# Eight instead of four PE transposes per PSUM tile and VectorE copy in a linear-attention and mixture-of-experts layer

## The reference

```python
qkv = silu(hidden_states @ qkv_w.T)
q, k, v = split(qkv.reshape(b, s, H, 3 * D), 3, axis=-1)   # blocks of 256 tokens
def step(state, blk):
    qi, ki, vi = blk
    aw = einsum('bhid,bhjd->bhij', qi, ki) * dd
    intra = einsum('bhij,bhjd->bhid', aw, vi)
    inter = einsum('bhid,bhde->bhie', qi * qd_, state)
    new_state = state * bd_ + einsum('bhsd,bhse->bhde', ki * kd_, vi)
    return (new_state, intra + inter)
attn = rmsnorm(attn, norm_w)
out = (sigmoid(hidden_states @ gate_w.T) * attn) @ out_w.T
```

## Time and profile before

| what | us |
|---|---|
| two timed runs | 5248.16 and 5294.14, median 5271.15 |
| the profiled execution, device time | 4658.65 |
| its span, slowest core (0) | 4656.1 |
| spans of the other cores | 4646.3 to 4655.0 |
| layer norm, from the first sum to the last copy (core 0) | 24 to 209 |
| the four groups | 209 to about 1245 |
| experts and store | about 1880 to 4656 |

### The profile page before, as it was taken

How to read it: one execution, slowest core, us unless ns; L and a number is a source line. 1 busy time by engine, 2 the same in 40 slices (tenths; PEclk the granted TensorE clock), 3 DMA queues, 4 the chain that set the end, 5 groups by cost and what they waited for, 6 DMA issues and landing times.

```text
span 4656.1 us, 43812 instructions; the slowest of 8 cores (4646.3 to 4656.1 us)
## 1 busy us (share of the span) xinstructions
PE 3917.6 (84%) x17686; PEld 1753.4 (38%) x18010; DVE 827.2 (18%) x1373; ACT 593.8 (13%) x691; POOL 251.0 (5%) x477
## 2 busy tenths in 40 slices
PE   1386876768649953999999999999999999999996
PEld 0132332323314421444444444444444444444443
DVE  3313122130222125011011011011011011010012
ACT  3311101111121030110110110110100100100100
POOL 0000000000000000000000000000000000000000
PEclk9996876868759965999999999999999999999997
DMA  3211111112103410444444444444444444444443
GB/s 104 68 32 19 31 29 20 31 19 50 32 0 64 72 54 14 73 73 77 74 75 74 77 73 74 76 73 76 75 73 77 73 73 73 77 73 77 75 71 95
DMA packets 75331, 284.48 MB, mean 61 GB/s; under 512 B 9814, under 2 KB 9975, under 8 KB 71038
## 3 DMA queue, kind: packets, MB, share of 16 engines
q0 software_dynamic: 67216, 243.39, 31.0%
q1 hardware_dynamic: 7918, 38.29, 2.3%
HBM read 516.55 MB, written 8.39 MB: 113 GB/s over the span
## 4 chain that ended last, share of the span: by engine, by line
PE 82%; DVE 8%; issue 4%; ACT 3%; DMA 2%; DVEq 0%; ACTq 0%; SPq 0%; POOL 0%; POOLq 0%
PE PD L368 28%; PE PE L368 27%; PE PD L1041 10%; PE PE L1041 9%; PE PT L383 2%; DVE awT L640 2%; DMA ring<-i_wup 1%; PE PC L654 1%; PE PE L654 1%; DVE statc L405 1%; PE PC L1077 1%; PE PC L812 1%; ACT R L447 1%; DVE k_tm L389 1%; ACT R L674 1%
## 5 line engine op out<-in xcount | busy, mean ns | idle before, releaser
L368 PE MATMUL PD<-R,ring 128*128 128x512 bf16 x5772 | 1314.0, 383 | 30.5 <-ACT R L998 10.8
L368 PE MATMUL PE<-R,ring 128*128 128x512 bf16 x5762 | 1299.6, 380 | 9.5 <-ACT bcB L772 1.3
L368 PEld LDWEIGHTS PD<-R,ring 128*128 128x128 bf16 x5888 | 580.1, 99 | 742.3 <-issue 70.5
L368 PEld LDWEIGHTS PE<-R,ring 128*128 128x128 bf16 x5888 | 577.4, 98 | 703.6 <-issue 17.2
L1041 PE MATMUL PD<-R,ring 128*128 128x512 bf16 x2008 | 458.6, 384 | 29.4 <-DVE R L1025 21.0
L1041 PE MATMUL PE<-R,ring 128*128 128x512 bf16 x2006 | 449.5, 379 | 3.1 <-DMA ring<-i_wdn 0.6
L1018 DVE TENSOR_TENSOR R<-R 128x1024 bf16<-128x1024 bf16 x128 | 88.6, 692 | 1628.2 <-ACT R L1011 1628.2
L1041 PEld LDWEIGHTS PD<-R,ring 128*128 128x128 bf16 x2048 | 201.1, 99 | 279.4 <-issue 48.7
L1041 PEld LDWEIGHTS PE<-R,ring 128*128 128x128 bf16 x2048 | 199.7, 98 | 243.9 <-issue 4.8
L998 ACT ACTIVATE R<-PD,bupP 128x1024 bf16<-128x1024 f32 x56 | 62.4, 1114 | 1050.4 <-PE PD L368 925.9
L383 PE MATMUL PT<-ident_b,R 128*128 128x128 bf16 x256 | 37.4, 301 | 154.7 <-ACT R L447 120.0
(11 more groups left out here) (168 smaller groups left out, 1633.5 us busy)
## 6 DMA issues: line engine op xcount, KB each, us to landing
ring<-i_wup POOLq DMA_DIRECT2D x112, 512.0 KB, 5.0
ring<-i_wgt POOLq DMA_DIRECT2D x112, 512.0 KB, 5.0
ring<-i_wdn POOLq DMA_DIRECT2D x112, 512.0 KB, 5.0
xstage<-i_xm SPq DMA_DIRECT2D x16, 1024.0 KB, 4.7
ring<-i_wk POOLq DMA_DIRECT2D x16, 512.0 KB, 5.0
xstage<-i_xp SPq DMA_DIRECT2D x8, 1024.0 KB, 4.8
ring<-i_wv POOLq DMA_DIRECT2D x16, 512.0 KB, 5.0
ring<-i_wq POOLq DMA_DIRECT2D x16, 512.0 KB, 5.0
```

Source lines behind the costliest of these rows:

```text
L368: t.matmul(P[:, hh * 512:(hh + 1) * 512], sl[:, kc * 128:(kc + 1) * 128], rb[:, kc * 1024 + hh * 512:kc * 1024 + (hh + 1) * 512], start=st ...
```

## The change

Every call of `transpose_batch` gets 8 pieces instead of 4, so that one batch fills `PT` and one DVE copy takes all of it. There are half as many batches. Nothing else differs. One of the three places in the groups and the layer norm:

```diff
-              for q4 in range(4):
+              for q8 in range(2):
                   transpose_batch(
-                      R3, [lo + (q4 * 4 + j) * 128 for j in range(4)], ("lntm", k), (),
-                      lambda tc=tc, q4=q4, dst=dst: dst.ap().rearrange(
-                          "p (fc t) -> p fc t", t=1024)[:, q4 * 4:(q4 + 1) * 4,
+                      R3, [lo + (q8 * 8 + j) * 128 for j in range(8)], ("lntm", k), (),
+                      lambda tc=tc, q8=q8, dst=dst: dst.ap().rearrange(
+                          "p (fc t) -> p fc t", t=1024)[:, q8 * 8:(q8 + 1) * 8,
                                                         tc * 128:(tc + 1) * 128],
                       dst_key, ident_b)
...
-        for mcl in range(4):
-            for q4 in range(2):
-                transpose_batch(
-                    k_fm, [mcl * 1024 + (q4 * 4 + j) * 128 for j in range(4)],
...
+        for mcl in range(4):
+            transpose_batch(
+                k_fm, [mcl * 1024 + j * 128 for j in range(8)],
+                ("kf", g, mcl), pref_done,
+                lambda mcl=mcl: k_tm.ap().rearrange(
+                    "p (tc j) -> p tc j", j=512)[:, 0:8,
+                                                 mcl * 128:(mcl + 1) * 128],
+                "ktm", ident_b)
```

More of the change, by code:

```diff
@@ L489, in build_nc @@
             evp = project(slab, skey, R2, "R2", tmp_fm, ("tm", mcl), mcl * 1024)
-            pend += [lambda q4=q4, mcl=mcl, evp=evp: transpose_batch(
-                tmp_fm, [mcl * 1024 + (q4 * 4 + j) * 128 for j in range(4)],
+            pend += [lambda mcl=mcl, evp=evp: transpose_batch(
+                tmp_fm, [mcl * 1024 + j * 128 for j in range(8)],
                 ("tm", mcl), (evp,),
-                lambda q4=q4, mcl=mcl: k_tm.ap().rearrange(
-                    "p (tc j) -> p tc j", j=512)[:, q4 * 4:(q4 + 1) * 4,
+                lambda mcl=mcl: k_tm.ap().rearrange(
+                    "p (tc j) -> p tc j", j=512)[:, 0:8,
                                                  mcl * 128:(mcl + 1) * 128],
-                "ktm", ident_b) for q4 in range(2)]
+                "ktm", ident_b)]
         for mcl in range(4):
@@ L505, in build_nc @@
             evp = project(slab, skey, R2, "R2", tmp_fm, ("tm", mcl), mcl * 1024)
-            pend += [lambda q4=q4, mcl=mcl, evp=evp: transpose_batch(
-                tmp_fm, [mcl * 1024 + (q4 * 4 + j) * 128 for j in range(4)],
+            pend += [lambda mcl=mcl, evp=evp: transpose_batch(
+                tmp_fm, [mcl * 1024 + j * 128 for j in range(8)],
                 ("tm", mcl), (evp,),
-                lambda q4=q4, mcl=mcl: v_tm.ap().rearrange(
-                    "p (tc j) -> p tc j", j=512)[:, q4 * 4:(q4 + 1) * 4,
+                lambda mcl=mcl: v_tm.ap().rearrange(
+                    "p (tc j) -> p tc j", j=512)[:, 0:8,
                                                  mcl * 128:(mcl + 1) * 128],
-                "vtm", ident_b) for q4 in range(2)]
+                "vtm", ident_b)]
         for th in pend:
@@ L559, in build_nc @@
         for mcl in range(4):
-            for q4 in range(2):
-                transpose_batch(
-                    k_fm, [mcl * 1024 + (q4 * 4 + j) * 128 for j in range(4)],
[L563 to L574, removed]
+            transpose_batch(
+                k_fm, [mcl * 1024 + j * 128 for j in range(8)],
+                ("kf", g, mcl), pref_done,
+                lambda mcl=mcl: k_tm.ap().rearrange(
+                    "p (tc j) -> p tc j", j=512)[:, 0:8,
+                                                 mcl * 128:(mcl + 1) * 128],
+                "ktm", ident_b)
+            transpose_batch(
+                q_fm, [mcl * 1024 + j * 128 for j in range(8)],
+                ("vmain", g, mcl), pref_done,
+                lambda mcl=mcl: v_tm.ap().rearrange(
+                    "p (tc j) -> p tc j", j=512)[:, 0:8,
+                                                 mcl * 128:(mcl + 1) * 128],
+                "vtm", ident_b)
         for tc in range(8):
```

## The result

| | before | changed |
|---|---|---|
| executions that the comparison uses, us | 4654.20 to 4665.18 (7) | 4584.98 to 4588.92 (4) |
| all timed executions, median us | 4661.87 (10) | 4785.58 (11) |
| profiled execution, us | 4658.65 | 4585.41 |
| spans of the eight cores, us | 4646.3 to 4656.1 | 4573.5 to 4583.9 |
| ratio of these | | 0.9843, 95% interval 0.9829 to 0.9857 |

The change makes the kernel faster by 1.57%, or 73 us of 4661, which is inside the 2% that I had called no difference to tell, though with this many executions it can be told. Some executions of either kernel show a lower mean granted clock on the cores of one die or both (0.77 to 0.89 instead of 0.90 or 0.91) and last up to 5382 us, and with 5248 and 5294 us both timed runs shown ahead of the prediction are of that length, so the ratio is the result and the medians are not.

A forecast was written before the change was run, and what follows sets the result against it. Experts set most of the time, but the change lies on PE and DVE taking turns: layer norm 20.6, k 11.4, v 10.3 and main runs 21.7 sum to 64.0 us, so 5271.15 becomes 5207 us, range 5162 to 5258.

The forecast's parts named there:

- the same 64 us: Layer norm and the groups' k, v and main runs: total saving from 96 removed batches, also subtracted from the timed median.
- A copy of eight: 690 ns: DVE's bf16 copy of eight pieces out of PSUM: 425 ns for four pieces plus 265 for four more.
- Rival 1: DVE's copy of eight goes at the f32 pace, 1224 ns; 17 us gained, 5254 us; chance 0.06.
- A pair saves 0.645: PE and DVE alternation: two turns of four become one turn of eight, saving 0.645 us at both of PE's paces.
- Layer norm 20.6: Layer norm: 16 turns of the loop, 2 pairs of batches each, at 0.645 us a pair, save 20.6 us.
- Rival 2: Layer norm does not follow, its turn set by the load or ACT's chain; 43 us gained, 5228 us; chance 0.05.
- k runs 11.4, v runs 10.3, main runs 21.7: Transpose runs of the four groups: savings in us at 0.645 a pair, with 1.1 for hidden last copies in k and main.
- The clock's part, costed at nothing: Projection behind the k run: avoiding PE's fall in pace might gain 5 us, a longer slow stretch lose 5; taken as nothing.
- Experts unchanged: Experts, which hold no transpose: their stretch of 1590 us was to stay the same.
- Rival 3: Dense stages: PE's pace drops because the program is denser ahead of them; at 3%, 118 us lost, 5325 us; chance 0.05.
- Rival 4: Timed runs gain more, by their longer turns (72 us) or a PE pace better by 1.6% (64 more): 5135 us; chance 0.07.

The follow-up runs named there:

- the last one: Against the changed kernel, batches of eight go in turn to PT and the first half of PA, another bank; ratio to before 0.9629.

## Why the prediction was right or wrong

*The time.* Wrong: 5207 us, range 5162 to 5258, for a kernel that takes 4585 to 4589 in the executions compared. The step that failed is "so I subtract the same 64 us: 5271.15 - 64.0 = 5207". I had seen that the profiled execution was 612.5 us shorter, that its eight cores agreed within 10 us, and that no row said where the rest was spent, and still took the two timed runs for the kernel's time. Seven of the ten executions of before are within 11 us of one another at 4654 to 4665 and the profiled one is among them. By the prediction's own sum against the profiled execution, the changed kernel was to take 4594.7; it took 4585.4. The change of within 2% was given the highest chance and came, but that says nothing for the time: 64 us are 1.2% of the one base and 1.4% of the other.

*The change.* Right in direction and mechanism, short in size: 64.0 forecast, 71.7 in the front, 12% more. Step by step:
- "A copy of eight: 690 ns": measured 692. Rival 1 (the f32 pace, 1224 ns) is out; it was given 0.06. What stood beside it from the Trainium skill's "VectorE: DVE Perf Modes", section "Mode 1× (REGULAR) — the baseline", taken as a rule for PSUM operands, doesn't hold for a bf16 copy of this size (692 ns, where as many f32 elements take 1224); the same page's section "Why PSUM operands drop a tier" does.
- "A pair saves 0.645": measured, turns of 2.02 and 1.61 us, as forecast. Its division misleads: I counted 160 ns of it as a copy's fixed part, and the run with two copies shows that a copy that has nothing to wait for costs only 0.07 us of them; the rest is paid because the copy stands in the round trip. This changes nothing in the sum, but it does in what one would do next.
- "Layer norm 20.6": 20.9. Rival 2, that its turn is set by something else, is out.
- "k runs 11.4, v runs 10.3, main runs 21.7": 12.6, 11.6, 22.2, each a little more. In the k and v runs PE had slowed for the last three or four of eight batches; now it slows for the last of four or for none. Each four transposes at the faster pace are 0.2 us shorter. I had this as "The clock's part, costed at nothing". The projection behind the k run, where I looked for it, still starts slow (8.32 us on core 0 before is 0.4 short for its missing record); from group to group it became 0.7 us longer to 1.7 shorter, 2 us less in all.
- Everything between the runs, which the sum put at nothing: about 5 us less, 2 in the kernel with the layer norm alone and 4 in the one with the groups alone. They are the 2 us behind the k runs, 1 us in the first projection behind the layer norm and 2 in the blocks, while the q projections lost 1 us. In the projections it is PE's pace in the first matmul group, since nearly all the others keep their length; what sets how long it stays low, and the cause in the blocks, stay open.
- Experts unchanged: the rest of the span, 3297.3 to 3298.5 us. Rival 3, slower in the dense stages because the program is denser ahead of them, is out: at 4585 us the changed kernel's mean granted clock is 0.909 against 0.905. Rival 4, a larger gain in longer executions, was built on the same mistaken time and wasn't tested.

The chances of 0.89 for within 2% and 0.09 for faster fit a ratio of 0.9843.

## What to carry to other kernels

A producer and a consumer that alternate on one tile pay a round trip a batch, here 0.57 us whatever the batch holds, so fill the tile; but a second tile in another bank is worth more than twice as large a batch (121 against 72 us), and both together most (157). Two tiles in one bank were not tried. Where short stretches of PE work stand ahead of dense ones, closing their gaps can also pay in the dense one's first microseconds (10 of the 85 us between the changed kernel and the last one). And when a profiled execution and the timed ones disagree by 13%, ask for more executions or forecast the difference against the profiled one, before working out tenths of a microsecond.

## What the runs showed that I had not expected

Two DVE copies from PSUM without a wait between them overlap: two of 425 ns fill 0.76 us. Where each copy waits for the one before it, because both write `k_tm`, they don't: in the k run with two tiles of four the starts of two such copies are 0.52 us apart (239.45 and 239.97, 240.58 and 241.10) for copies of 0.42. The wait takes 0.1 us and the overlap away. It is the same wait that makes a turn 1.33 us instead of 1.26 in the run with eights in the layer norm alone.

PE's pace rose inside a run of nothing but 128 x 128 transposes, from 1.01 to 0.61 us for eight (107 to 55 ns a step), once the gaps between them were gone. With gaps of 1 us between batches of eight, and also with two tiles of four, it stayed at the slower pace to the end of the main run.
